# Four-layer kernel: the attention's key product folded into one matrix, the experts' down-projection made token-major

## The reference, cut to what matters

```python
# c
qkv = jnp.einsum('btc,cd->btd', x, W) + b
q, k, v = jnp.split(qkv, 3, axis=-1)
weights = jnp.einsum('btc,bTc->btT', q, k) * scale
attention = softmax(where(tril, weights, -9e15))
values = jnp.einsum('btT,bTc->btc', attention, v)
# d
g = jax.nn.silu(jnp.einsum('th,efh->tef', x, w1_e))
u = jnp.einsum('th,efh->tef', x, w3_e)
routed = jnp.einsum('tef,ehf,te->th', g * u, w2_e, combine)
shared = _swiglu(x, w1_s, w3_s, w2_s)
```

## Time and profile before

| | |
|---|---|
| Median of 3 runs (lowest, highest) | 707.75 us (706.18, 711.22) |
| The profiled execution | 708.59 us, span from the first to the last instruction 706.8 us |
| Mean granted TensorE clock | 0.973 of 2.4 GHz |
| Busy, share of the span | PE 94%, PEld 72%, DVE 83%, ACT 68%, POOL 44% |

### The profile page before, as it was taken

How to read it: one execution, slowest core, us unless ns; L and a number is a source line. 1 busy time by engine, 2 the same in 40 slices (tenths; PEclk the granted TensorE clock), 3 DMA queues, 4 the chain that set the end, 5 groups by cost and what they waited for, 6 DMA issues and landing times.

```text
span 706.8 us, 11728 instructions
## 1 busy us (share of the span) xinstructions
PE 662.7 (94%) x3654; PEld 510.9 (72%) x3654; DVE 585.6 (83%) x1873; ACT 479.4 (68%) x974; POOL 310.7 (44%) x793
## 2 busy tenths in 40 slices
PE   3778789999999999999999999999999999999994
PEld 2566677777868787777868787787868787766652
DVE  1566798889898998889898988889898988977772
ACT  2245476686877868786877868786877868666542
POOL 1336443345354535345354535445454535431311
PEclk9778899999999999999999999999999999999997
...
DMA packets 18686, 12.69 MB, mean 18 GB/s; under 512 B 704, under 2 KB 18240, under 8 KB 18368
## 3 DMA queue, kind: packets, MB, share of 16 engines
...
...
## 4 chain that ended last, share of the span: by engine, by line
PE 88%; ACT 4%; DVE 3%; POOL 2%; issue 1%; DMA 1%; SPq 0%; ACTq 0%; DVEq 0%; POOLq 0%
PE bank L552 17%; PE bank L346 11%; PE bank L348 10%; PE bank L347 10%; PE bank L355 10%; PE bank L462 2%; PE bank L435 2%; PE bank L406 2%; PE bank L479 2%; PE bank L425 2%; PE bank L473 2%; PE bank L474 2%; PE bank L450 2%; PE bank L519 2%; PE bank L500 1%; PE bank L506 1%
## 5 line engine op out<-in xcount | busy, mean ns | idle before, releaser
L552 PE MATMUL bank<-hid,whole 128*128 128x512 f32 x288 | 146.8, 594 | 0.3 <-DVE hid L1360 0.3
L346 PE MATMUL bank<-x3T_hi,w_hi 128*128 128x512 f32 x288 | 138.1, 480 | 0.1
L903 ACT ACTIVATE silu<-bank 128x512 f32<-128x512 f32 x144 | 86.3, 599 | 75.8 <-PE bank L348 72.9
L1350 DVE TENSOR_TENSOR gu<-silu,bank 128x512 f32<-128x512 f32 x128 | 86.7, 677 | 32.6 <-ACT silu L903 17.8
L348 PE MATMUL bank<-x3T_hi,w_lo 128*128 128x512 f32 x288 | 113.6, 394 | 0.0
L1632 POOL TENSOR_TENSOR moment<-stats 128x4 f32<-128x4 f32 x192 | 46.5, 274 | 151.9 <-DVE stats L1164 124.6
L347 PE MATMUL bank<-x3T_lo,w_hi 128*128 128x512 f32 x288 | 112.7, 391 | 0.0
L1360 DVE TENSOR_TENSOR hid<-gu,bank 128x512 f32<-128x512 f32 x128 | 87.3, 682 | 3.2 <-PE bank L552 1.8
L346 PEld LDWEIGHTS bank<-x3T_hi,w_hi 128*128 128x128 f32 x288 | 54.2, 188 | 28.7 <-issue 9.6
L1618 POOL TENSOR_TENSOR qk<-rope_c,rope_s 128x512 f32<-128x512 f32 x32 | 40.6, 1277 | 75.4 <-DVE rope_s L1126 75.4
L1632 POOL TENSOR_TENSOR rstd<-moment,whole 128x4 f32<-128x4 f32 x64 | 64.8, 1012 | 5.0
...
## 6 DMA issues: line engine op xcount, KB each, us to landing
...
```

The source lines that it names most:

```text
L346: mm(out, wh, mh, start=True, stop=False)
L552: mm(YB[:], whole[:, a:a + P], hid[:, c % 2], start=c == 0, stop=c == CHUNKS).then_inc(p_w2.sem, 1)
L903: fn(silu[:, c % 2], GB[:], ACT.Silu).then_inc(a_silu.sem, 1)
L1350: tt(gu[:, c % 2], silu[:, c % 2], UB[:], ALU.mult).then_inc(v_gu.sem, 1)
```

## The change

Keys. With q = x Wq + bq and k = x Wk + bk, a score is x M x' plus one term that depends on the key alone, one that depends on the query alone, and a constant. `fold_keys` makes M = Wq Wk' (times the scale) and the vectors for these terms on the chip, once, in `first_turns`: two transposes, four small fp32 products, five ACT copies, and three DVE operations in `fold_bias`. `c_project` makes one product (M, into B1) where it made two; the keys' operand in `c_scores` is x2T itself. The term that depends on the query alone is a 129th column of `c_value`'s product; `c_value` now has two halves, two tiles in B0 and two in B1, on PE and on DVE. The maximum is handled in two steps: DVE's `c_max` takes the plain maximum of each row, and POOL's new `c_shift` adds the query's term and subtracts it again, the result being the bias of the exponentials. `c_scores` waits for each half's `v_cv`; before, it waited for it ahead of the second sequence only.

Down-projection. `d_down` has the activations stationary: 4 products per chunk, each with a tile of `hid` as weights and 128 columns of w2 as moving operand, so that YB is token-major. `d_y` on ACT, `d_yT` on PE and the tile yT are gone; `d_res` reads YB after the last `d_down`. ACT's `c_norm` has a new wait, for `d_res` two blocks back, since x3 has two buffers.

Orders. All five lists of PE, ACT, DVE and POOL are reordered. The turns are shown whole; of the first and last turns, the pieces that are spoken of.

```diff
+def fold_keys():
+    nc.tensor.transpose(B0[:, 0:P], raw("cq"), ident)
+    nc.tensor.transpose(B0[:, P:2 * P], raw("ck"), ident).then_inc(p_fold.sem, 1)
+    pe.wait_ge(a_fold.sem, 1)
+    pe.wait_ge(v_fold.sem, 3)
+    wqT, wkT = foldT[:, 0:P], foldT[:, P:2 * P]
+    mm(B1[:, 0:P], wqT, wkT, start=True, stop=True)
+    mm(B1[:, P:P + 1], wkT, const("bcq"), start=True, stop=True)
+    mm(B1[:, P + 1:P + 2], wqT, const("bck"), start=True, stop=True)
+    mm(B1[:, P + 2:P + 3], const("ones"), b_qk[:], start=True, stop=True).then_inc(p_fold.sem, 1)
 def c_project(n):
+    if not started(n):
+        pe.wait_ge(a_fold.sem, 5)
     pe.wait_ge(a_xT[2].sem, a_xT[2].at(n))
-    mm(B1[:], raw("cq"), xT[2][:], start=True, stop=True).then_inc(p_cq.sem, 1)
-    mm(B0[:], raw("ck"), xT[2][:], start=True, stop=True).then_inc(p_ck.sem, 1)
-def c_value(n):
-    pe.wait_ge(a_cq.sem, a_cq.at(n))
-    for t in range(TILES):
-        last = mm(tile(B1, t), tile(xT[2], t), raw("cv"), start=True, stop=True)
+    mm(B1[:], m_qk[:], xT[2][:], start=True, stop=True).then_inc(p_cq.sem, 1)
+def c_value(n, half):
+    pe.wait_ge(a_xT[2].sem, a_xT[2].at(n))
+    if half == 1:
+        pe.wait_ge(a_cq.sem, a_cq.at(n))
+    b = B1 if half else B0
+    for i in range(2):
+        last = mm(b[:, i * SEQ:i * SEQ + CVW], tile(xT[2], 2 * half + i), w_cv[:], start=True, stop=True)
     last.then_inc(p_cv.sem, 1)
 def c_scores(n):
-    pe.wait_ge(a_ck.sem, a_ck.at(n))
     for s, b in ((0, B0), (1, B1)):
-        if s == 1:
-            pe.wait_ge(v_cv.sem, v_cv.at(n))
+        pe.wait_ge(v_cv.sem, v_cv.at(n, s + 1))
         q0, q1 = tile(cqT, 2 * s), tile(cqT, 2 * s + 1)
-        k0, k1 = tile(ckT, 2 * s), tile(ckT, 2 * s + 1)
+        k0, k1 = tile(xT[2], 2 * s), tile(xT[2], 2 * s + 1)
         mm(b[:, 0:P], ident_b[:], causal_b[:], start=True, stop=False)
         mm(b[:, 0:P], q0, k0, start=False, stop=True)
...
     if c == 0 and started(n):
         pe.wait_ge(v_res[3].sem, v_res[3].at(n - 1))
     a = CONST_COLS["w2"][0] + c * P
-    mm(YB[:], whole[:, a:a + P], hid[:, c % 2], start=c == 0, stop=c == CHUNKS).then_inc(p_w2.sem, 1)
-def d_yT(n):
-    pe.wait_ge(a_y.sem, a_y.at(n))
-    transpose_tiles(YB, lambda t: tile(yT, t), ident).then_inc(p_yT.sem, 1)
+    for t in range(TILES):
+        last = mm(tile(YB, t), tile(hid[:, c % 2], t), whole[:, a:a + P], start=c == 0 and t == 0, stop=c == CHUNKS and t == TILES - 1)
+    last.then_inc(p_w2.sem, 1)
 def turn(i, odd, load=None):
     a, b, c, d, e = live(i), live(i - 1), live(i - 2), live(i - 3), live(i - 4)
     if a: a_xT_(i, odd, load)
     if d: d_hidden(i - 3, 1 - odd, 0)
+    if c: c_scores(i - 2)
+    if a: a_vT_(i)
     if d: d_cT(i - 3)
-    if c: c_scores(i - 2)
-    if e: d_yT(i - 4)
-    if a: a_vT_(i)
     if d: d_hidden(i - 3, 1 - odd, 1)
     if c: c_pT(i - 2)
     if a: a_qk(i)
+    if d: d_down(i - 3, 0)
+    if b: b_xT(i - 1)
     if c: c_av(i - 2)
-    if b: b_xT(i - 1)
+    if a: a_v_(i)
+    if b: b_small(i - 1)
+    if d: d_hidden(i - 3, 1 - odd, 2)
     if a: a_g_(i)
-    if d: d_down(i - 3, 0)
-    if b: b_small(i - 1)
-    if a: a_v_(i)
-    if d: d_hidden(i - 3, 1 - odd, 2)
+    if d: d_hidden(i - 3, 1 - odd, 3)
+    if a: a_qT_(i)
     if a: a_kv(i)
-    if a: a_qT_(i)
-    if d: d_hidden(i - 3, 1 - odd, 3)
+    if d: d_hidden(i - 3, 1 - odd, 4)
     if d: d_down(i - 3, 1)
-    if d: d_hidden(i - 3, 1 - odd, 4)
     if a: a_num_(i)
     if d: d_down(i - 3, 2)
     if c: r_xT(i - 2, odd)
-    if d: d_down(i - 3, 3)
     if d: d_hidden(i - 3, 1 - odd, 5)
     if c: r_gate(i - 2)
     if b: b_dnT(i - 1)
+    if d: d_down(i - 3, 3)
+    if a: a_aT(i)
+    if b: b_up(i - 1)
     if d: d_down(i - 3, 4)
-    if b: b_up(i - 1)
+    if first_turn(i): fold_keys()
     if d: d_hidden(i - 3, 1 - odd, 6)
+    if a: a_out(i)
     if d: d_down(i - 3, 5)
-    if a: a_aT(i)
     if d: d_hidden(i - 3, 1 - odd, 7)
     if d: d_down(i - 3, 6)
     if d: d_hidden(i - 3, 1 - odd, 8)
     if b: c_xT(i - 1)
-    if a: a_out(i)
     if d: d_down(i - 3, 7)
     if b: c_project(i - 1)
+    if b: c_value(i - 1, 0)
     if d: d_down(i - 3, 8)
-    if b: c_value(i - 1)
+    if b: c_value(i - 1, 1)
...
-    a_qT_(0)
     a_num_(0)
+    fold_keys()
     a_aT(0)
     a_xT_(1, 1, 0)
...
+    c_av(0)
+    a_v_(2)
     b_xT(1)
-    c_av(0)
     a_g_(2)
     a_qT_(2)
-    a_v_(2)
     b_small(1)
+    a_kv(2)
+    a_num_(2)
     r_xT(0, 0)
-    a_kv(2)
     r_gate(0)
     b_dnT(1)
+    a_aT(2)
     b_up(1)
-    a_num_(2)
+    a_xT_(3, 1, 1)
     d_hidden(0, 0, 0)
-    a_aT(2)
+    a_out(2)
     d_hidden(0, 0, 1)
...
     d_hidden(13, 1, 0)
     c_scores(14)
-    d_yT(12)
     d_cT(13)
+    d_hidden(13, 1, 1)
     c_pT(14)
-    d_hidden(13, 1, 1)
     c_av(14)
     b_xT(15)
     d_down(13, 0)
     b_small(15)
...
+def fold_keys():
+    act.wait_ge(p_fold.sem, 1)
+    fn(foldT[:], B0[:, 0:2 * P], ACT.Copy).then_inc(a_fold.sem, 1)
+    act.wait_ge(p_fold.sem, 2)
+    fn(m_qk[:], B1[:, 0:P], ACT.Copy, scale=C_SCALE).then_inc(a_fold.sem, 1)
+    fn(r_b[:], B1[:, P:P + 1], ACT.Copy, scale=C_SCALE).then_inc(a_fold.sem, 1)
+    fn(w_cv[:, P:CVW], B1[:, P + 1:P + 2], ACT.Copy, scale=C_SCALE).then_inc(a_fold.sem, 1)
+    fn(b_cv[:, P:CVW], B1[:, P + 2:P + 3], ACT.Copy, scale=C_SCALE).then_inc(a_fold.sem, 1)
...
-def c_qkv(n):
+def c_query(n):
+    if not started(n):
+        act.wait_ge(a_fold.sem, 5)
     act.wait_ge(p_cq.sem, p_cq.at(n))
-    fn(cqT[:], B1[:], ACT.Identity, scale=C_SCALE, bias=bcq_s[:]).then_inc(a_cq.sem, 1)
-    act.wait_ge(p_ck.sem, p_ck.at(n))
-    fn(ckT[:], B0[:], ACT.Identity, bias=const("bck")).then_inc(a_ck.sem, 1)
+    fn(cqT[:], B1[:], ACT.Identity, bias=r_b[:]).then_inc(a_cq.sem, 1)
 def c_exp(n):
     for s, b in ((0, B0), (1, B1)):
-        act.wait_ge(v_max.sem, v_max.at(n, 2 * s + 2))
+        act.wait_ge(g_max.sem, g_max.at(n, 2 * s + 2))
...
 def turn(i, odd):
     a, b, c, d, e = live(i), live(i - 1), live(i - 2), live(i - 3), live(i - 4)
+    if a: x0_hi(i)
     if d: d_silu(i - 3, 0)
-    if a: x0_hi(i)
-    if second(i): split_late()
     if c: c_exp(i - 2)
     if a: a_vT_(i)
     if c: c_pT(i - 2)
     if d: d_silu(i - 3, 1)
     if b: copy_xT(i - 1, 1, B0)
+    if a: a_tap0(i)
     if b: b_small(i - 1)
+    if a: a_v_(i)
+    if d: d_silu(i - 3, 2)
     if a: a_g_(i)
-    if a: a_v_(i)
-    if a: a_tap0(i)
-    if d: d_silu(i - 3, 2)
+    if d: d_silu(i - 3, 3)
     if a: a_qT_(i)
-    if d: d_silu(i - 3, 3)
-    if b: b_exp(i - 1)
     if c: c_norm(i - 2, odd)
     if d: d_silu(i - 3, 4)
+    if b: b_exp(i - 1)
     if c: r_hi(i - 2, odd)
-    if d: d_silu(i - 3, 5)
     if c: r_exp(i - 2)
     if b: b_dnT(i - 1)
+    if d: d_silu(i - 3, 5)
+    if e: e_norm(i - 4)
     if d: d_silu(i - 3, 6)
-    if e: e_norm(i - 4)
     if d: d_silu(i - 3, 7)
+    if second(i): split_late()
     if b: b_layer_norm(i - 1)
+    if first_turn(i): fold_keys()
     if d: d_silu(i - 3, 8)
     if b: copy_xT(i - 1, 2, B0)
-    if b: c_qkv(i - 1)
-    if d: d_y(i - 3)
+    if b: c_query(i - 1)
...
+def fold_bias():
+    tt(b_qk[:], const("bcq"), const("bck"), ALU.mult).then_inc(v_fold.sem, 1)
+    nc.vector.tensor_copy(w_cv[:, 0:P], w_raw[:, WEIGHT_COLS["cv"][0]:WEIGHT_COLS["cv"][1]]).then_inc(v_fold.sem, 1)
+    nc.vector.tensor_copy(b_cv[:, 0:P], const("bcv")).then_inc(v_fold.sem, 1)
...
         dve.wait_ge(p_s.sem, p_s.at(n, s + 1))
         for i, (a, w) in enumerate(((0, P), (P, 2 * P))):
-            red(neg_max[:, 2 * s + i:2 * s + i + 1], b[:, a:a + w], AX.X, ALU.max, negate=True).then_inc(v_max.sem, 1)
-def c_value(n):
-    dve.wait_ge(p_cv.sem, p_cv.at(n))
-    tt(cv[:], tiles(B1[:]), const("bcv").unsqueeze(1).broadcast_to([P, TILES, P]), ALU.add).then_inc(v_cv.sem, 1)
+            red(top_s[:, 2 * s + i:2 * s + i + 1], b[:, a:a + w], AX.X, ALU.max).then_inc(v_max.sem, 1)
+def c_value(n, half):
+    if not started(n):
+        dve.wait_ge(a_fold.sem, 5)
+    dve.wait_ge(p_cv.sem, p_cv.at(n, half + 1))
+    tt(cv[:, 2 * half:2 * half + 2], by_tile(B1 if half else B0)[:, :, 0:CVW],
+       b_cv[:].unsqueeze(1).broadcast_to([P, 2, CVW]), ALU.add).then_inc(v_cv.sem, 1)
 def d_res(n, odd):
     if started(n):
         dve.wait_ge(a_x4.sem, a_x4.at(n - 1))
-    dve.wait_ge(p_yT.sem, p_yT.at(n))
+    dve.wait_ge(p_w2.sem, p_w2.at(n))
     tt(res[3][:], x3[odd][:], tiles(YB[:]), ALU.add).then_inc(v_res[3].sem, 1)
...
 def turn(i, odd):
     a, b, c, d, e = live(i), live(i - 1), live(i - 2), live(i - 3), live(i - 4)
+    if c: c_max(i - 2)
     if d: d_gu(i - 3, 0)
-    if c: c_max(i - 2)
+    if e: d_res(i - 4, odd)
     if d: d_hid(i - 3, 0)
     if b: a_layer_norm(i - 1)
-    if e: d_res(i - 4, odd)
     if a: a_rope(i)
+    if second(i): split_late()
+    if d: d_gu(i - 3, 1)
     if c: c_res(i - 2)
-    if d: d_gu(i - 3, 1)
-    if b: b_norm(i - 1, 0)
     if d: d_hid(i - 3, 1)
     if d: d_gu(i - 3, 2)
+    if a: conv_tap(i, 1)
+    if b: b_norm(i - 1, 0)
+    if d: d_hid(i - 3, 2)
```

(104 more changed lines are left out.)

291 lines of the change are left out of this document (148 added, 143 removed).

## The result

The changed kernel takes 696.98 us (median of 4 runs, 695.52 to 697.5) against 707.02 us (median of 4) before: ratio 0.984, 95% interval 0.982 to 0.986. That is 10.0 us faster where 17.8 were forecast: within the stated range of 684 to 703 us, and 7 us above the forecast of 690. The profiled execution took 695.52 us (span 693.7), the fastest of its four, and that of before 708.59, above its median, so the two profiles lie 13.1 us apart: 3 us of what the profiles show is spread of the runs.

The account below looks back on a forecast made before the run. PE was taken to bound the turns, a microsecond of its work being one of time. Twelve turns -12.4, head -2.3 and tail -3.1 sum to -17.8 us, from 707.75 to 690 us; range 684 to 703.

Parts of the forecast that it names:

- the walk: One turn followed in the new order through PE's pieces and DVE's starts: no stall found, so zero for waits.
- Rival 1: Every d_down: weight loads of the token-major product not hidden, 779 us with nothing hidden; chance 0.05.
- rival 2: Turns: DVE becomes the bound, the turn stays at 39.8 us, only head and tail gain, 702 us; chance 0.13.
- rival 3: Turns: the three tightest places (c_pT, a_v, a_aT) miss, 0.5 us per turn, 696 us; chance 0.17.
- Rival 4: Head: it gains more because the filled wait for x3 is kept, 686 us; chance 0.08.
- Head: -2.3 forecast: Stretch up to turn 4's first transpose: 2.3 us shorter, bounds -4.3 and -0.8.
- The start of d_hidden(0,0), booked as zero: Head: first expert product starts about where it did, at 85.45 us; bounds -2 and +1.5.
- The terms -0.88 -1.72 +0.27: Head, PE after d_hidden(0,0): a_aT(2) and a_xT(3) already past, two key products gone, nine d_down costing more, in us.
- After it PE is nearly gapless: Head: after d_hidden(0,0) PE has almost no idle time, so its smaller work was counted as time, -2.3 us.
- Tail: -3.1 forecast: Stretch after the twelve turns: 3.1 us shorter, within 1.5 either way.
- d_yT not hidden: -1.4: Tail's end: the last output transposes and their copy go, so the last d_res waits for PE alone, -1.4 us.
- -0.86 -1.32 +0.8 -0.3: Tail, in us: block 15's key product gone, d_yT of blocks 12 to 14 gone, 27 d_down dearer, c_pT(14)'s wait filled.

Follow-up runs that it names:

- e3: Both parts of the change (token-major down-projection and folded key product) in the orders of the kernel before: 712.37 us, ratio 1.007.
- e6: The changed kernel with the down-projection's weights stationary again, still without copy and transposes, so its output is not the sublayer's: 693.32 us, ratio 0.977.
- e9: The changed kernel with the old down-projection, its copy and transposes, so the new orders with the folded key product alone: 700.91 us, ratio 0.988.
- e10: The kernel before, with neither part of the change, in the changed kernel's orders: 711.57 us, ratio 1.003.
- e1: The kernel before, in its own orders, with the token-major down-projection alone: 710.92 us, ratio 1.005.
- e2: The kernel before, in its own orders, with the folded key product, halved c_value and c_shift alone: 714.93 us, ratio 1.009.
- e5: Both parts in the orders of the kernel before, with four moves in the steady turn on PE and ACT: 710.63 us, ratio 1.002.
- e7: The changed kernel with two moves in DVE's order before the steady turns (block 0's routing groups, block 1's row maxima earlier): 697.48 us, ratio 0.983.
- e11: The changed kernel with short products of two constants filling 18 of PE's waits before the steady turns: 695.04 us, ratio 0.980.
- e12: e11 with more filling products at two places, without c_shift and the 129th column, and with e7's moves: 692.74 us, ratio 0.978.
- e4: The changed kernel without c_shift, DVE writing the negated maximum itself: 696.7 us, ratio 0.984.
- e8: e4 with the tail reordered: a down-projection of block 13 and block 15's second value product, scores and exponentials moved earlier: 695.68 us, ratio 0.981.

## Why the forecast was right, and where it was 7 us off

**Turns: right in the mechanism.** Forecast 38.77 us, measured 38.88; twelve turns give -11.1 for -12.4. d_down cost 0.89, and the old key product and yT left in full. Of the missing 0.11 us, 0.05 is one of the nine down-projections, which adds 0.94, and 0.06 is a small wait that the walk did not list: the folded product adds 0.92 for 0.86. In the new order only a down-projection stands between c_xT and c_project, where a_out stood there as well, and the load of the product begins at 323.72, right behind the end of ScalarE's copy of x2T (323.07 + 0.60):

```profile
323.07 0.60 ACT L838 ACTIVATE x2T<-bank 128x512 f32<-128x512 f32 x1 [0.54 <-PE bank L367]
...
323.72 0.30 PEld L499 LDWEIGHTS bank<-x2T,m_qk 128*128 128x128 f32 x2
...
323.76 1.08 PE L499 MATMUL bank<-x2T,m_qk 128*128 128x512 f32 x2
```

In e3, with the old order, the product adds 0.86. In e6, e9 and e10, in the new order, the trace names the wait of the load for x2T (0.66 us), and the product adds 0.95. The other pieces move a little with the order and nearly cancel.

Rival 1 is settled by e6 (0.03 us per chunk, decisive only at 0.15), rival 2 by e6's shorter turn, rival 3 by the absence of waits at c_pT, a_v and a_aT; two taps of the convolution in a row took 1.53 us in this turn, and the 1.96 us did not come back. Rival 4 falls with the head, below. That rival 3's price of 696 us is nearly the time that came out is chance. So is, in part, that the range held: its upper end stood at 703 us for rival 2, which did not come, while the forecast with head and tail at their bounds reaches 693.

**What the prediction did not say** is that the parts alone are worth nothing. It priced them as PE's work, which holds only where PE has enough of its own work beside each chain that leaves it and comes back, and that the new orders provide. e1, e2, e3 and e10 show that neither the parts nor the orders give anything by themselves; e9 shows the fold worth 0.75 us per turn in the new orders, and the token-major form 0.13 more. The walk had looked at the new order alone, which is why its answer holds for it. Two of these chains were followed in a trace, x0T to x0T_lo and the scores to probT (e3, e5); that the others work alike is an inference.

**Head: -2.3 forecast, -0.8 measured.** The windows from the first expert product to turn 4, before and after the change:

```profile
85.45:133.09 47.64, 45.68 (x257) 34.05 (x256) 42.61 (x145) 29.79 (x62) 22.18 (x60) 1.00 0.04 12
```

```profile
86.06:132.28 46.22, 43.73 (x296) 37.49 (x297) 40.36 (x145) 28.07 (x59) 21.88 (x63) 1.00 0.04 13
```

Three steps gave less than forecast. The start of d_hidden(0,0), booked as zero, came 0.61 us later (86.06 for 85.45, within 83 to 87): the mix ended at 83.36 and not near 82.5 as walked, and POOL's a_gate and x3_lo, 1.27 and 1.26 us, stand behind it. The terms -0.88 -1.72 +0.27 promise 2.33 us less work; PE's busy time fell by 1.95. And "After it PE is nearly gapless" took new waits for nothing, where PE's idle time grew by 0.53 us (2.49 for 1.96). Together that is +0.61 -1.95 +0.53 = -0.81 us. DVE is busy 9.21 of the 10 us from 90 us on and PE 8.13; that DVE's order is to blame was my next theory, and e7 did not bear it out. By e10's profile the new orders, which were booked with a gain of 0.88 us there, cost 2.1. e11, with the clock at 0.95 instead of 0.89 from 15 to 112 us, starts the turns no earlier, and how much each of e12's edits does in the head stays open.

**Tail: -3.1 forecast, -1.2 measured** (598.79 to the end, for 610.73 before), outside its bound of 1.5 either way. "d_yT not hidden: -1.4" came true (the last stretch, from block 15's combine weights to the last d_res, is 20.96 us for 22.18, with 9 x 0.03 added in it). Wrong was to book PE's work ahead of it (-0.86 -1.32 +0.8 -0.3) as time. The windows up to block 15's combine weights, before and after:

```profile
610.73:675.42 64.69, 62.88 (x307) 43.55 (x307) 51.02 (x163) 40.26 (x80) 18.26 (x59) 1.00 0.02 5
```

```profile
598.79:663.64 64.85, 61.62 (x400) 52.45 (x399) 50.66 (x164) 39.96 (x79) 19.30 (x66) 1.00 0.03 9
```

PE's work fell by 1.26 us, its idle time grew by 1.42, and the stretch did not become shorter. Most of that lies beside block 15's chain from its key product to its combine weights, 31.9 us for 31.7, at whose end PE waits 0.76 us. e4, without `c_shift`, shortens the chain to 31.3; e8, which moves PE's waits, does not shorten it further.

**The profiles.** The remaining 3 us are no step of the sum: the profiled run of the changed kernel is the fastest of its four, and that of before lies 1.6 us above the median. e11's four runs and e12's six agree within 0.6 us each, with the head's clock held up in part or wholly, where the changed kernel's four spread over 2.0; this suggests that most of the spread arises there. If it does so in the kernel before as well, the head is not shorter at all by the medians: 10.0 us less the turns' 11.1 and the tail's 1.2 leave it some 2 us longer. No second profile of either kernel shows it.
